# Second layer of a two-layer cross-attention kernel: the weighted sum moved ahead of scores and transposes, the division ahead of the softening

## What is computed

```python
scores = jnp.einsum('bhqd,bhkd->bhqk', q, k) / jnp.sqrt(jnp.float32(HD))
scores = scores * mask - 10000.0 * (1.0 - mask)
probs = jax.nn.softmax(scores, axis=-1)
return jnp.einsum('bhqk,bhkd->bhqd', probs, v)
```

## Time and profile before

| | |
|---|---|
| three timed runs | 2162.21, 2168.14, 2183.37 us; median 2168.14 |
| the profiled execution | 2166.06 us, of which the span is 2164.3 us |
| mean granted TensorE clock in it | 0.946 |
| second layer's attentions | about 919 us to 1765 us from the span's start |

### The profile page before, as it was taken

The page is one execution under the profiler, slowest core; times in us unless marked ns, Lnnn a source line. Parts: engine busy times, 40 slices in busy tenths (PEclk is TensorE's granted clock), DMA queues, the critical chain, the costliest instruction groups (busy, mean ns, idle before and its releaser), DMA issues. The chain is left out here.

```text
span 2164.3 us, 32608 instructions
## 1 busy us (share of the span) xinstructions
PE 1916.0 (89%) x12032; PEld 1209.6 (56%) x12032; DVE 1213.3 (56%) x2735; ACT 1054.4 (49%) x2298; POOL 137.8 (6%) x95
## 2 busy tenths in 40 slices
PE   3779999999999986488999999999989758999999
PEld 2324333343433332366776767767766438999998
DVE  6666575757665521156676666766666346433332
ACT  1346555555665452164666666666656344111111
POOL 3010010101000000001000000000000000100000
PEclk8779999999999988789999999999999879999999
DMA  5222222222122200835455555454541424000000
GB/s 157 81 74 70 70 75 80 65 76 74 61 72 54 60 2 19 274 91 123 118 129 132 131 123 128 103 149 106 142 103 40 112 56 136 32 28 20 20 20 20
DMA packets 159374, 185.36 MB, mean 86 GB/s; under 512 B 25072, under 2 KB 115312, under 8 KB 159216
## 3 DMA queue, kind: packets, MB, share of 16 engines
q1 hardware_dynamic: 159216, 183.27, 31.4%
HBM read 119.78 MB, written 63.44 MB: 85 GB/s over the span
## 5 line engine op out<-in xcount | busy, mean ns | idle before, releaser
L734 DVE TENSOR_REDUCE a_mx<-a_mscore 128x2 f32<-128x1024 f32 x256 | 313.1, 1223 | 265.0 <-PE a_mscore L427 264.8
L583 ACT ACTIVATE a_pt<-a_escore 128x1024 f32<-128x1024 f32 x256 | 261.8, 1023 | 216.5 <-PE a_escore L415 215.6
L1393 ACT ACTIVATE b_pr<-b_t,b_nmax 128x256 f32<-128x256 f32 x512 | 253.8, 499 | 183.2 <-DVE b_nmax L1503 183.2
L1499 DVE TENSOR_TENSOR b_t<-b_score,b_mask 128x1024 f32<-128x1024 f32 x128 | 156.0, 1219 | 157.8 <-PE b_score L1281 157.7
L1503 DVE CUSTOM_DVE_ANT_0 b_t<-b_t,b_minus 128x256 f32<-128x256 f32 x512 | 196.7, 440 | 16.9
L427 PE MATMUL a_mscore<-a_kst,a_qst 48*128 48x512 f32 x512 | 135.2, 524 | 60.5 <-DVE a_mx L734 49.2
L1820 ACT ACTIVATE c_gT<-c_d,c_b 128x256 f32<-128x256 f32 x128 | 53.7, 471 | 264.9 <-PE c_d L1745 264.8
L1405 ACT ACTIVATE b_pt<-b_d 128x512 f32<-128x512 f32 x256 | 139.0, 592 | 79.2 <-PE b_d L1293 73.9
L427 PEld LDWEIGHTS a_mscore<-a_kst,a_qst 48*128 48x128 f32 x512 | 50.8, 193 | 223.5 <-issue 128.6
L1293 PE MATMUL b_d<-b_ident,b_pr 128*128 128x128 f32 x1024 | 142.8, 280 | 19.7 <-DVE b_cxT L1523 8.0
L415 PE MATMUL a_escore<-a_qst,a_kst 50*128 50x512 f32 x512 | 129.5, 502 | 23.5 <-ACT a_pt L583 23.4
(11 more groups left out here) (137 smaller groups left out, 3328.8 us busy)
## 6 DMA issues: line engine op xcount, KB each, us to landing
b_qst<-b_q SPq DMA_DIRECT2D x96, 256.0 KB, 5.1
b_kst<-b_k SPq DMA_DIRECT2D x96, 256.0 KB, 7.2
b_q<-b_parts SPq DMA_DIRECT2D x64, 256.0 KB, 2.8
b_k<-b_parts SPq DMA_DIRECT2D x64, 256.0 KB, 2.8
a_qst<-a_q_parts SPq DMA_DIRECT2D x192, 64.0 KB, 2.2
a_kst<-a_k_parts SPq DMA_DIRECT2D x192, 64.0 KB, 2.2
a_q_parts<-a_qparts SPq DMA_DIRECT2D x32, 256.0 KB, 2.3
a_k_parts<-a_kparts SPq DMA_DIRECT2D x32, 256.0 KB, 2.4
```

Of the source, the lines that this page charges most:

```text
L583: nc.scalar.activation(pt[:, at % RING, :, :], escore[:], ACT.Exp, scale=SCALE).then_inc(exp_done.sem, 1)
L734: nc.vector.tensor_reduce(mx[:, q, 2 * pair:2 * pair + 2], mscore[:], AX_X, ALU.max).then_inc(max_done.sem, 1)
L1393: last = nc.scalar.activation(pr[:, u % 2, j, :], t[:, u % 2, j, :], ACT.Exp, scale=-1.0, bias=nmax[:, u, j:j + 1], accum_out=esum[:, u, j ...
L1499: nc.vector.tensor_tensor(t[:, u % 2], score[:, u % 2].rearrange("p x (y n) -> p (x y) n", y=2), mask[a][:, q, :].unsqueeze(1).broadcast_t ...
```

## The change

In TensorE's body `weigh` of the preceding unit becomes the first step of a position; before it was the third, behind `scores` and `turn_probs`. The list of bank uses follows that order. In VectorE's body `divide` of the preceding unit comes ahead of `soften`; before it came behind it. ScalarE, GpSimd and SyncE keep their programs; no instruction is added or removed.

```diff
         for p in POSITIONS:
             a, shift, u = unit_at(0, p)
-            uses += [(("pt", a, u, k), shift) for k in range(TT)]
+            turned = [(("pt", a, u, k), shift) for k in range(TT)]
             a, shift, u = unit_at(0, p - 1)
-            uses += [(("w", a, u), shift)]
-            uses += FILL[p]
+            uses += [(("w", a, u), shift)] + turned + FILL[p]
...
             def body(i):
                 for p in POSITIONS:
+                    weigh(i, *unit_at(i, p - 1))
                     scores(*unit_at(i, p + 2))
                     turn_probs(i, *unit_at(i, p))
-                    weigh(i, *unit_at(i, p - 1))
                     fill(i, p)
...
             def body(i):
                 for p in POSITIONS:
+                    divide(*unit_at(i, p - 1))
                     soften(*unit_at(i, p + 2))
-                    divide(*unit_at(i, p - 1))
                     invert(*unit_at(i, p + 1))
```

## The result

The changed kernel takes 2194.95 us (median; 2193.39 to 2202.14) against 2166.16 us before: a ratio of 1.0138, 95% interval 1.0106 to 1.0169, so it is slower by 1.1% to 1.7%. Its profiled execution took 2193.49 us, 27.4 us more than the one of before; the forecast was 18.1 us more.

What follows compares the result with a forecast made beforehand. TensorE bounds steady turns, except where scores, softening, exponentials and emptying stall it. Terms 3.5 + 4.7 - 0.9 + 8.3 + 2.5 = 18.1 us on 2166.06 give 2184; own range 2174 to 2195, overall 2160 to 2203.

Steps and rivals of the forecast that it cites:

- Position 9 and position 1: Stalled projections start later because scores come 0.79 us later: +0.50 us at seven places (3.5), +0.79 at six (4.7).
- Position 14: Stalls on `lnT` now have `weigh` inside them, while `lnT` may come later: -0.15 us six times, -0.9 us.
- Everywhere else in a steady turn TensorE itself is the limit: Outside the stalled places of a steady attention turn, TensorE sets the pace and absorbs the 0.79 us: no cost.
- The clock: Longer stalls at positions 1 and 9 bring more falls to 1.2 GHz: five more, +8.3 us, ends -5 and +16.6.
- A mean clock in the steady turns no lower than before: Sign of a wrong prediction: steady attention turns show a mean clock no lower than in the kernel before; no size.
- The ends: In positions without fill, `weigh` waits for ScalarE's copies while some waits for divisions go: +2.5 us, between -12.7 and +8.
- `divide` charged at nothing: On VectorE, `divide` ahead of `soften`, about 0.6 us, runs while TensorE does the scores: zero.
- Entering `weigh` behind a fill: On TensorE, `weigh` inherits the wait for the fill's last matmul and scores lose it: zero, plus or minus 17 us.
- the rival of a costly entry: `weigh` pays in full for starting behind fills and scores keep their cost: +17 us more, 2201; chance 0.12.
- division first: At the layer's ends, 12.7 us of TensorE's waits for divisions go unreplaced: 2160.7, faster than before; chance 0.1.
- nothing moves: VectorE or ScalarE hides the 0.79 us at both stalled places; ends and clock cancel: 2166; chance 0.08.
- The delay without more clock falls: Stalls at positions 1 and 9 grow but clock falls are no more frequent than now: 2176; chance 0.2.

Runs made afterwards that it cites:

- the run without falls and collision: Changed kernel with GpSimd's addition held until position 5's softening and two unused matmuls added in each of the two stalls; 2178.70 us, ratio 1.0074.
- ScalarE's edit: Kernel before, with ScalarE emptying the transposed inputs ahead of the exponentials at positions 0, 8 and 13 instead of behind them; 2146.69 us, ratio 0.9925.

## Why the prediction was right or wrong

The direction was right, and so was the main mechanism: a later softening makes the stalls at positions 1 and 9 longer, and at the ends `weigh` waits for copies. The total, 2194.95 us, is only just inside the forecast's own range of 2174 to 2195. On the profiled executions the size was short by 9.3 us, 27.4 in place of 18.1. The chance of a difference within 1%, put at 0.67, went to the wrong side: the slowdown is 1.1% to 1.7%, which had 0.3. That the sum came near is partly luck, since the clock was put far too high, the ends too low and the collision at nothing. By its own steps:

**Position 9 and position 1** (+0.50 and +0.79 us a turn). From its transposes to its projection position 9 takes 5.37 us (1155.56 to 1160.93) against 4.79: +0.58. From the transposes of position 0 to the output projection, in a turn without a fall, it is 11.86 us against 10.89: +0.97. Right, a little low. In the first full turn position 1 adds only 0.05 us.

**Position 14** (-0.15). 7.62 us (1187.56 to 1195.18) against 7.69: -0.07. Right. The three sum to 1.48 us a turn where 1.14 was forecast; the run without falls and collision has 1.4 to 1.8. Over the steady stretch, place by place, they give 4.9 (position 1), 3.5 (position 9) and -0.1 (position 14), 8.3 us of the 15.1.

**"Everywhere else in a steady turn TensorE itself is the limit", and the 0.79 us absorbed.** This step failed. The softening of position 3 slid into GpSimd's addition, which before fell beside `negative`. Three turns waited 1.24, 1.22 and 1.37 us and were 1.5 to 1.7 us longer for it, 4.6 us in all, and moving the addition took those waits away. The prediction used just this contention at position 12, where it is in the rows, and never asked what the delay would bring together elsewhere.

**The clock** (+8.3). Mis-sized, and the largest error of the sum. A fall costs 1.68 us, close to the 1.66 taken. But from the first full turn to position 13 of i = 5 the changed kernel's profiled execution has five falls and the one of before three. One of the five lies across the start of the first full turn (1009.2), which is only 0.6 us longer than before, no more than its two chains. That leaves one fall, +1.7 us, and not +8.3. The stalls grew to 2.05 and 1.9 us unbroken, where 2.4 and 2.0 were forecast. A fall followed three of the five long position-1 stalls, as many as before, and two of the seven at position 9, where none did before; the forecast had them in most turns at position 1 and in about half at position 9. A mean clock in the steady turns no lower than before was one of the prediction's signs of being wrong, and it came: 0.99 in both over the four turns. How often falls come belongs to the execution as much as to the kernel: the run with the addition moved had two of them in some turns. The Trainium skill ("TensorE: Matmul & The Clock Gate", "What's actually happening"), cited in the prediction, says that the number of slow matmuls varies from run to run, and the trace agrees: the changed kernel's four executions have mean clocks from 0.936 to 0.943. Filling the stalls removed the falls, so the link between stall and fall is shown.

**The ends** (+2.5). Mis-sized: 8.5 us, just outside the end of 8, and 1.7 us more for the fall in the output projection behind them. The mechanism was the one named, `weigh` waiting for its own unit's copies with scores and transposes behind it. The divisions' 12.7 us of waits did go but for 1.8, and 18.9 us of waits for copies took their place. The run with the old order at the ends shows it: 7.0 us come back. In the last cross-attention a position takes 3.80 to 4.22 us (`weigh` at 1765.36, 1769.16, 1773.00, 1777.22, 1781.40) where 3.8 was forecast, and the sum did not follow `lnT`, for which the transposes wait 4.4 us in place of 1.3.

**`divide` charged at nothing.** Right for the pair, incomplete as a reading. The new list makes a transposed input claim the bank of `weigh`. That it costs nothing in the steady turns is owed to the division going first; the prediction did not see that the two halves need each other (29 us against 69).

**Entering `weigh` behind a fill** (zero). Right: 5.79 us against 5.80 for a position. `weigh` takes 0.79 us to the scores behind it in the changed kernel (1204.59 to 1205.38, behind a fill), as it took before behind transposes. So the rival of a costly entry gave nothing here, and with it the reason that the prediction took from the Trainium skill ("TensorEngine Tiling (Array Packing)", "Key Properties"): no run shows a position made longer by it. The rival "division first" had its 12.7 us go but be replaced; "nothing moves" fell with the first chain. "The delay without more clock falls", 2176, had the clock nearly right and lacked the collision and the ends.

Sum of what the traces show: 8.3 + 4.6 + 1.7 steady (14.6, measured 15.1), 0.8 at the start of the stage, 8.5 at the ends, 1.7 for the fall in the last output projection, and 1.4 in the first layer, which the change does not touch and which is the difference between two executions.

## What to carry to other kernels

Where an in-order engine reads results two steps ahead, do first what frees a bank or a buffer for someone who waits, and last what is needed only later. Moving emptyings ahead of exponentials gained 0.75%, and twice applied 1.95%, with no instruction removed; moving `weigh` ahead of scores did the opposite and lost 1.4%, together with what it brought along elsewhere. When an edit delays a chain by less than a microsecond, look not only for who waits in it but for what else on another engine it will now coincide with. A reordering of a ring of buffers changes who claims the late one: list these claims for both orders before counting any time.

## What was not expected of the hardware

A custom instruction of VectorE on SBUF takes 0.42 us alone and 2.58 us when GpSimd's 2.5 us addition has started just before it: it ends only 0.29 us behind the addition. The same addition beside VectorE's `negative` made that one 2.30 us where it takes 0.39 alone (1129.47 in the changed kernel), so the cost is the same and only its place counts.

A fall of the granted clock costs the same 1.7 us in the three kernels where like turns differ by falls alone: 1.68 us in the kernel before, 1.69 in it with ScalarE's edit (99.11 against 97.42), 1.68 in the changed kernel with the addition moved. Keeping TensorE busy with work that no result uses, 1.7 us in each stall, left no fall in the four turns compared. Such work was worth at most what the falls cost; taking the stall itself away was worth both.
